# A Chebyshev graph layer and a SAGE layer on one core: holding GpSimd to three indexed loads under way, with a semaphore for each row group of a wide strip

## The reference

```python
def _L0_gnn_ref(x, L, weight):            # L = adj, K = 4
    terms = [x, L @ x]
    for _ in range(2, K):
        terms.append(2.0 * (L @ terms[-1]) - terms[-2])
    return jnp.einsum('kni,kio->no', jnp.stack(terms, axis=0), weight)

def _L1_gnn_ref(X, adj, W, b):
    deg = jnp.clip(jnp.sum(adj, axis=1, keepdims=True) + 1.0, 1.0, None)
    h_neigh = (adj @ X + X) / deg
    out = jax.nn.relu(jnp.concatenate([X, h_neigh], axis=1) @ W + b)
    return out / jnp.maximum(jnp.linalg.norm(out, axis=1, keepdims=True), L2_EPS)

h = jnp.maximum(_layernorm(x, axis=-1), 0.0)
x = x + _L0_gnn_ref(h, adj, L0_gnn_weight)
h = jnp.maximum(_layernorm(x, axis=-1), 0.0)
x = x + _L1_gnn_ref(h, adj, L1_gnn_W, L1_gnn_b)
```

## Time and profile before

| | before |
|---|---|
| median of three runs | 2425.84 us |
| the profiled execution, its own time | 2429.75 us |
| its span from first to last instruction | 2427.9 us |
| TensorE matmuls busy | 2100.9 us (87%) |
| VectorE busy | 1660.0 us (68%) |
| ScalarE busy | 688.5 us (28%) |
| GpSimd busy | 1347.6 us (56%) |
| moved by DMA | 702.67 MB, mean 289 GB/s |
| mean granted TensorE clock | 0.939 of full speed |

### The profile page before, as it was taken

How to read it: one execution, slowest core, us unless ns; L and a number is a source line. 1 busy time by engine, 2 the same in 40 slices (tenths; PEclk the granted TensorE clock), 3 DMA queues, 4 the chain that set the end, 5 groups by cost and what they waited for, 6 DMA issues and landing times.

```text
span 2427.9 us, 29911 instructions
## 1 busy us (share of the span) xinstructions
PE 2100.9 (87%) x12104; PEld 1645.1 (68%) x12104; DVE 1660.0 (68%) x1260; ACT 688.5 (28%) x1667; POOL 1347.6 (56%) x1437
## 2 busy tenths in 40 slices
PE   2788889999999989999999867687888999977776
PEld 1455567788888867878888655566777777845554
DVE  7776887577776547665766454764666768588787
ACT  2444332443433146212123443511112221200010
POOL 5666665556555256357655262525574756667761
PEclk9898999999999999999999988888999999988898
DMA  9999999989988769689988787658896999999995
GB/s 280 365 359 347 352 350 361 327 294 347 326 295 305 240 170 297 235 290 299 321 268 308 218 227 235 203 179 291 262 278 219 362 323 339 305 363 318 300 261 155
DMA packets 225099, 702.67 MB, mean 289 GB/s; under 512 B 48834, under 2 KB 79554, under 8 KB 224962
## 3 DMA queue, kind: packets, MB, share of 16 engines
q0 software_dynamic: 168192, 664.89, 81.4%
q1 hardware_dynamic: 51776, 34.64, 5.7%
q10 hardware_dynamic: 4994, 1.25, 0.4%
HBM read 698.55 MB, written 2.10 MB: 289 GB/s over the span
## 4 chain that ended last, share of the span: by engine, by line
PE 72%; DVE 16%; DMA 4%; issue 3%; ACT 3%; POOL 2%; SPq 0%; DVEq 0%; ACTq 0%
PE ps_pair L736 51%; PE ps_single L742 14%; DVE ring L621 11%; DMA ring<-in_adj_dram,index 3%; ACT ring L441 2%; POOL ring L392 2%; PE ps_lin L700 1%; PE ps_lin L699 1%; PE ps_lin L684 1%; PE ps_lin L690 1%; PE ps_lin L695 1%; PE ps_lin L687 1%; PE ps_tr L703 1%; ACT sum_p L462 0%; DVE vec L491 0%
## 5 line engine op out<-in xcount | busy, mean ns | idle before, releaser
L392 POOL DMA_INDIRECT ring<-in_adj_dram,index x1424 | 1346.0, 945 | 1026.9 <-issue 402.9
L621 DVE STREAM_TRANSPOSE ring<-ring 128x2048 f32<-128x2048 f32 (+7 forms) x742 | 1478.9, 2053 | 164.0 <-ACT ring L441 142.0
L736 PE MATMUL ps_pair<-ring,vec 128*128 128x256 f32 x5760 | 1315.9, 389 | 108.2 <-DVE ring L621 83.2
L736 PEld LDWEIGHTS ps_pair<-ring,vec 128*128 128x128 f32 x5760 | 1109.5, 195 | 302.4 <-issue 111.1
L742 PE MATMUL ps_single<-ring,vec 128*64 128x256 f32 x4864 | 611.2, 405 | 183.5 <-DVE ring L621 177.8
L441 ACT ACTIVATE ring<-ring 128x1024 f32<-128x1024 f32 (+7 forms) x736 | 576.7, 787 | 432.9 <-DMA ring<-in_adj_dram,index 432.4
L742 PEld LDWEIGHTS ps_single<-ring,vec 128*64 128x64 f32 x4864 | 358.5, 145 | 405.8 <-issue 194.0
L460 ACT ACTIVATE sum_s<-ps_single 128x512 f32<-128x512 f32 x76 | 45.2, 594 | 932.4 <-PE ps_pair L736 469.4
L552 DVE TENSOR_TENSOR row_sums<-row_sums,more_sums 128x16 f32<-128x16 f32 x30 | 5.3, 178 | 312.5 <-PE ps_lin L696 166.3
L441 ACT ACTIVATION_READ_ACCUMULATOR ring<-ring 128x1 f32 x736 | 139.4, 189 | 0.0
L556 DVE TENSOR_TENSOR res<-res,ps_lin 128x256 f32<-128x256 f32 x16 | 6.7, 418 | 126.4 <-PE ps_tr L703 116.8
(11 more groups left out here) (79 smaller groups left out, 519.3 us busy)
## 6 DMA issues: line engine op xcount, KB each, us to landing
ring<-in_adj_dram,index POOLq DMA_INDIRECT x1424, 7.1
ring<-in_adj_dram SPq DMA_DIRECT2D x160, 96.0 KB, 2.7
ring<-in_adj_dram SPq DMA_DIRECT2D x160, 64.0 KB, 3.7
ring<-in_adj_dram SPq DMA_DIRECT2D x160, 32.0 KB
out_dram<-vec SPq DMA_DIRECT2D x64, 32.0 KB
res<-in_x_dram SPq DMA_DIRECT2D x4, 256.0 KB, 7.6
res<-in_x_dram ACTq DMA_DIRECT2D x4, 256.0 KB, 8.5
tmp<-in_L_gnn_weight_dram ACTq DMA_DIRECT2D x2, 64.0 KB
```

Source lines behind the costliest of these rows:

```text
L392: pool.indirect_dma_start(strip_of(i)[:, g, :], None, adj_q, bass.IndirectOffsetOnAxis(ap=index[:, 0:1], axis=0), element_offset=(QN * (g ...
L621: nc.vector.transpose(blocks, blocks).then_inc(s_turned, 1)
L736: last = nc.tensor.matmul(ps_pair[n % 2][:, cells], vec[:, CB * J + c, :, :], moving, start=(pair == 0), stop=(pair == pairs - 1))
```

## The change

GpSimd keeps a queue of the loads that it has issued and not yet waited for. Once it holds three, GpSimd waits before each further load until the oldest of them has landed. A load's landing must be seen by itself for this, so each of the eight row groups of a strip gets its own semaphore in place of one for each pair (48 in place of 24), and a consumer that waited once for a pair now waits for two semaphores, one for each row group. This adds 1421 waits on GpSimd, one for each load but the first three, 712 on VectorE and up to as many on ScalarE. The loads, their sizes, their order and all computation stay as they are, and so do the narrow strips on SyncE.

```diff
+UNDER_WAY = 3
...
             k = wide_strips.index(i)
-            return s_wide[k % NSEM][p], 16 * 2 * (k // NSEM + 1)
+            return s_wide[k % NSEM][2 * p + 1], 16 * (k // NSEM + 1)
+
+        def landed(i, g):
+            k = wide_strips.index(i)
+            return s_wide[k % NSEM][g], 16 * (k // NSEM + 1)
...
-        s_wide = [[sem(f"wide_strip_loaded{i}_{p}") for p in range(PAIRS)] for i in range(NSEM)]
+        s_wide = [[sem(f"wide_strip_loaded{i}_{g}") for g in range(GH)] for i in range(NSEM)]
...
+            under_way = collections.deque()
             for i in wide_strips:
                 n, h, J0, w = strips[i]
                 if free_at[i] > 0:
                     pool.wait_ge(s_unit, free_at[i])
                 for g in range(GH):
+                    if len(under_way) == UNDER_WAY:
+                        pool.wait_ge(*under_way.popleft())
+                    under_way.append(landed(i, g))
                     at = CB * rows[n].C + CB // H * h + g // Q
                     pool.indirect_dma_start(
                         strip_of(i)[:, g, :], None, adj_q,
                         bass.IndirectOffsetOnAxis(ap=index[:, 0:1], axis=0),
                         element_offset=(QN * (g % Q) + 32 * at) * N + J0 * UC)\
-                        .then_inc(s_wide[wide_strips.index(i) % NSEM][g // 2], 16)
+                        .then_inc(s_wide[wide_strips.index(i) % NSEM][g], 16)
...
                     for p in range(steps_of[i]):
+                        if not narrow[i]:
+                            act.wait_ge(*landed(i, 2 * p))
                         act.wait_ge(*loads_of(i, p))
...
                 for p in range(steps_of[i]):
+                    if not narrow[i]:
+                        dve.wait_ge(*landed(i, 2 * p))
                     dve.wait_ge(*loads_of(i, p))
```

More of the change, by code:

```diff
@@ L36 @@
+import collections
 import itertools
```

## The result

The changed kernel takes 2929.99 us (median of four runs, 2923.58 to 2937.64) beside 2426.56 for the kernel before: 1.2077 times as long, 95% interval 1.2063 to 1.2091. I had forecast 2655 us with 2830 as the upper end. The sign was right and the size was not: +503 us instead of +229. The profiled execution took 2923.58 us; its span is 2921.8 us, 494 more than before.

The account below looks back on a forecast made before the run. Transfers were taken to bound the first stage, TensorE several later ones, and loads the last four; stage losses of 87 + 30 + 43 + 44 + 15 + 16 = +235 us gave 2661, stated as 2655 us, range 2515 to 2830.

Parts of the forecast that it names:

- What bounds the kernel, and the first stage: Sweep 1's first nine rows, 15 to 445 us: transfers set the pace, 1.47 us a load; forecast loss +87 us.
- The 9 under way in the first stage: First stage before the change: landing time 13.1 us over spacing 1.47 us gives 9 loads under way.
- The formula of the wait: GpSimd's indexed loads: spacing becomes (landing time + 0.3) / 3, or 1.24 us if that is longer.
- L at w = 8: Time from issue to landing of a width-8 indexed load, three under way: taken as 5.0 us, spacing 1.77.
- The cover that wasn't there: TensorE's three stages between 445 and 1230 us: loads already ahead cover half of the 60 us, leaving +30.
- The stages put at nothing: 1385 to 1680 us (2.17 us a load) and 1680 to 1865 (1.70): enough room, so no loss.
- the same list of stages: Stage-by-stage sum of losses from 15 to 2376 us: 87 + 30 + 43 + 44 + 15 + 16 = +235 us.
- The other edits: Further waits on VectorE and ScalarE and a semaphore for each load: taken to cost nothing, at most 214 us of VectorE's time.
- The one that stays at its high end: Rival: landing time 5.8 us at width 8, spacing 2.03, about +550, 2980 us; chance 0.07.
- Saturated engines: Rival: queued loads cover GpSimd's start, width-8 loads keep 1.47 us; 2426 to 2450 us; chance 0.08.
- Faster transfers: Rival: fewer loads under way keep the 16 engines in step at 415 GB/s; 2340 us; chance 0.05.
- signs that I named: Profile after: landing about 5 us, first stage some 90 us later, DMA share below 0.9, about 300 GB/s, TensorE near 2100 us.

Follow-up runs that it names:

- e1: Changed kernel with the limit at 100000, so GpSimd never waits for a landing; 2706.41 us, ratio 1.0012 to the kernel before in its group.
- e2: Changed kernel with the limit at sixteen instead of three loads under way; 2708.83 us, ratio 1.0018 to the kernel before in its group.
- e8: Changed kernel with the limit at eight instead of three loads under way; 2425.39 us, ratio 1.0006 to the kernel before in its group.
- e11: Changed kernel with the limit at six instead of three loads under way; 2422.86 us, ratio 0.9994 to the kernel before in its group.
- e4: Changed kernel with the limit at two instead of three loads under way; 3855.0 us in one run, the kernel before 2704.05 in that group.
- e5: The changed kernel again, limit at three, beside the kernel before; 2916.68 us, ratio 1.2032.
- e3: Changed kernel with the limit at four instead of three loads under way, single run; 2625.38 us, the kernel before 2704.05 in that group.

## Why the prediction was wrong in size

**What bounds the kernel, and the first stage.** Right. Transfers set the first stage and GpSimd's spacing rules it after the change. The 9 under way in the first stage fit too: with a limit of eight 105 of its 291 loads had to wait for a landing, with sixteen one of all 1424. But most of the nine were not needed, as a limit of five costs 0.3%.

**The formula of the wait.** Right. (L + 0.3) / 3 with the measured 5.6 gives 1.97 us, and the first stage has 585 / 292 = 2.00. A load starts 0.26 us after the landing that it waited for in the trace's semaphore events, near the 0.3 that I took.

**The step that failed: L at w = 8.** I took 5.0 us between 4.5 (a load after idle time) and 5.8 (the second to fourth loads, up to three ahead); it measured 5.6. The other widths were right within 0.1 (4.4 for 4.5 at w = 4, 4.8 for 4.8 at w = 6). My reason for the value was that with fewer under way queueing falls. But the row at the upper end was already close to the state asked for: those loads had one to three ahead of them, and with the limit at three a load has two. Where such rows exist, few as they are, the value lies at theirs and not in the middle. With 2.0 in place of 1.77 the first stage gives 292 x 2.0 - 430 = +154, and that is what was measured (+155). 784 of the 1424 loads have this width, and the loss is a difference of near numbers: 0.23 us more a load makes the spacing 13% longer and the stage's loss 77% larger (154 for 87).

**The cover that wasn't there.** From 445 to 1230 I halved +60 to +30, as loads ahead would cover a part. Measured to the same loads, these stages cost 79 less 20 (given back in the stretch of 810 to 870, where GpSimd had a long wait), 21 and 32 us, together 112. With the spacings as measured the sum for them is 73 + 13 + 29 = 115. So of 132 us lost only the 20 came back, and not half. I had counted on loads that are ahead when a stage begins. But the stage before these was bound by loads as well, so that none were ahead: between 600 and 1045 us of the changed kernel GpSimd waits 221.3 us for landings and only 9.9 us for TensorE's units, where it waited 101.2 us for them before.

**The stages put at nothing.** From 1010 to 1050, 1230 to 1385, 1385 to 1680 and 1680 to 1865 the changed kernel lost 12 + 27 + 5 + 17 = 61 us. The first two stages stand neither in the earlier trace rows nor in my list, though TensorE was full in the second of them; before and after:

```profile
1230.00:1385.00 155.00, 152.68 (x761) 130.91 (x759) 92.57 (x60) 49.56 (x135) 68.87 (x74) 1.00 0.86 285
1509.00:1693.00 184.00, 154.91 (x707) 128.30 (x707) 93.44 (x56) 50.30 (x142) 68.60 (x74) 0.91 0.78 238
```

A mean spacing of 155 / 74 = 2.09 us hides bursts: before, 68 of these 74 loads followed the one ahead by GpSimd's gap of 0.3 us, and all of them had started by 1346.6 us. Afterwards 63 of them wait for a landing, 75.4 us in all. That the 27 us come from these bursts is argued from this and was not tried by itself.

**The sum again.** With the spacings as measured (2.0, 1.79, 1.68 and 1.57 us for w of 8, 7, 6 and 4 or 5) and no cover, the same list of stages gives 154 + 73 + 13 + 29 + 67 + 56 + 18 + 18 = +428; with the 61 above, less the 20 given back, it is +469. Measured to the last load the loss is 513 us, and 19 of them come back behind it, as there is less left to do when it lands: 494 in the spans. The 44 us between 469 and 513 are spread; the two last stages hold 19 of them, as they lost 26 and 29 us where the list has 18 and 18. So of the 259 us by which 494 exceeds my 235, some 163 are the longer L, 30 the cover, 41 the stages at nothing less what was given back, and 25 stay unexplained. Two slips of the prediction change little: the low end at w = 6 was given as 4.5 us, which makes a spacing of 1.60 and not 1.55 (some 4 us in the sum), and the last three stages have 220 loads, not 218, which makes at most 27 us and not 24.

**The other edits** were put at nothing, and that was right (e1 and e2 1.0012 and 1.0018, e8 and e11 1.0006 and 0.9994).

**The rivals.** The one that stays at its high end, to which I gave 0.07, was the right one: its 2.03 us a load and 2980 us stand beside 2.00 and 2930. Saturated engines would have needed L = 4.1. Faster transfers appear at no limit that was run more than once. Most signs that I named came out, stronger than I said: median landing 5.4 us for about 5, the first stage 155 us later for some 90, a DMA share of 0.81 and 261 GB/s where I said below 0.9 and about 300. One did not: TensorE's busy time did not stay near 2100 us but grew by 138, although the same 12104 matmuls ran. In the first stage the granted clock fell from 0.94 to 0.85, and a slower matmul counts as more busy time.

## What to carry to other kernels

A kernel needs as many transfers under way, n, as bring (landing time with n under way + wake-up) / n down to the spacing that the bound allows. The wake-up is what passes from a landing to the start of the load that waited for it. Here four give (6.2 + 0.26) / 4 = 1.62 us and five (7.0 + 0.26) / 5 = 1.45, where the bound allows 1.47; so five are enough, a limit one lower costs 4%, and two lower 20%. The landing time of the unlimited kernel (13.1 us) is no guide, since most of it is queue. A load's landing time does not shrink in proportion when the queue is shortened, since most of it (4.4 of 5.6 us) is there when the load is alone; the loads that start after idle time give its low end, and the two or three issued right behind them are nearest to the state with the limit. When a resource is held by a round trip, cost it by loads of one size and in stretches no longer than its bursts, as means over a stage with room hide the part that is lost.

## What the runs showed of the hardware that was not expected

The kernel before took 2427 us in the first comparison and 2424 and 2423 in two groups of runs, but 2704 us in the group of e1 to e4 (19 runs, 2693.84 to 2710.59), 11% more. In that group the kernel with a limit of four took 2625 us in its one run, 3% less than the kernel before beside it, while elsewhere the same kernel took 4% more. The record has the same chip number for e1 to e4 as for e5 to e8, so that it isn't shown that another chip is the reason, though the expectation of e5 calls it one.

The transfers themselves were not the cause: the packets of the indexed loads took 74.2% of e1's 2708.0 us, 2009 us of all 16 engines, and 81.4% of 2427.9 before, 1976 us. TensorE's time is what grew. It was busy for 2218.3 us, 117 more than before, at a lower clock (0.899 for 0.939), and its waits grew by some 160 us, most of which stand in front of matmuls that wait for no semaphore. In e1 it stops twice for over 2 us in a run of such matmuls:

```profile
57.74 0.58 PE L757 MATMUL ps_single<-ring,vec 128*64 128x256 f32 x1 [2.43 <-issue]
60.53 2.01 PE L757 MATMUL ps_single<-ring,vec 128*64 128x256 f32 x8 [2.20 <-issue]
```

The same matmuls go without a stop in e8, from the second group:

```profile
53.72 4.54 PE L757 MATMUL ps_single<-ring,vec 128*64 128x256 f32 x40
```

Added up over the matmuls without a wait, such gaps are 134 us in e1, 50 in e3 and nothing in e4, e8, the changed kernel and the kernel before. The traces of this group also lack semaphore events, and in the same order: e1 has 17883 landing events where the kernel before has 31658, e3 has 22935 and e4 29938. So a cause that both share, the recording of the events among them, is as open as any other. Rows of waits that are put down to "issue" can't be trusted there, as a part of them has a releaser that was lost. What makes the group slow stays open, and so does whether a limit of four or five would be faster there if it were run more than once. A limit that is tried in one such group alone can come out with either sign.
